# Where the scale and shift of two layer norms are worked out in a one-core attention and experts kernel

## What is computed

```python
def _layernorm(x, axis=-1, eps=1e-05):
    m = jnp.mean(x, axis=axis, keepdims=True)
    v = jnp.var(x, axis=axis, keepdims=True)
    return (x - m) / jnp.sqrt(v + eps)
...
x = x + jnp.tanh(g_xattn[0]) * _L0_xattn_ref(_layernorm(x, axis=-1), ctx_1024, ctx_1024, mask, Wq, Wk, Wv, Wo, 16)
x = x + jnp.tanh(g_ffn[0]) * _L0_ffn_ref(_layernorm(x, axis=-1), Wg, bg, W1, b1, W2, b2)
```

## Time and profile before

| | us |
|---|---|
| median of 3 runs | 1108.44 |
| lowest and highest run | 1108.04, 1109.18 |
| the profiled execution's own time | 1107.66 |
| its span on the core | 1105.6 |

### The profile page before, as it was taken

One profiled execution on the slowest core, in us unless ns is written; L12 is line 12 of the kernel. 1 busy time (PEld: TensorE's weight loads), 2 busy tenths in 40 slices (PEclk: granted clock), 3 DMA queues, 4 the chain that ended last, 5 costly groups with the idle time before them and its releaser, 6 DMA issues.

```text
span 1105.6 us, 36301 instructions
## 1 busy us (share of the span) xinstructions
PE 1024.9 (93%) x13797; PEld 755.4 (68%) x13797; DVE 894.4 (81%) x1803; ACT 943.1 (85%) x1809; POOL 791.7 (72%) x719
## 2 busy tenths in 40 slices
PE   5868799999999999999999999999999999999887
PEld 4446567776777777677777767777776777777655
DVE  2686688897888889788888978888897888787766
ACT  3988788889898888989888898988889898887865
POOL 3566667776867777686777768777776877788843
PEclk9999899999999999999999999999999999999999
DMA  9122121212112121211212121121212111111100
GB/s 219 33 56 59 49 56 43 55 45 59 50 40 57 52 57 43 59 50 40 57 52 56 43 59 50 40 57 52 54 45 59 50 31 46 44 40 50 29 3 20
DMA packets 123162, 56.90 MB, mean 51 GB/s; under 512 B 26584, under 2 KB 122864, under 8 KB 122992
## 3 DMA queue, kind: packets, MB, share of 16 engines
q1 hardware_dynamic: 122992, 54.59, 19.3%
HBM read 16.80 MB, written 4.19 MB: 19 GB/s over the span
## 4 chain that ended last, share of the span: by engine, by line
PE 49%; DVE 14%; ACT 12%; issue 12%; POOL 11%; DMA 1%; ACTq 0%; DVEq 0%; SPq 0%; POOLq 0%
PE bank L44 15%; PE bank L46 14%; PE bank L45 14%; POOL hidL L895 3%; POOL ptL L932 3%; ACT qH L464 3%; POOL rstd L880 3%; PE bank L307 2%; ACT bank L520 2%; PE bank L262 2%; DVE shift L668 2%; ACT x2hat L508 1%; DVE comb L868 1%; ACT vH L559 1%; DVE above L844 1%
## 5 line engine op out<-in xcount | busy, mean ns | idle before, releaser
L895 POOL TENSOR_TENSOR hidL<-hid,hidH 128x512 f16<-128x512 f32 x242 | 278.6, 1164 | 21.3 <-ACT hidH L494 21.3
L932 POOL TENSOR_TENSOR ptL<-pt,ptH 128x512 f16<-128x512 f32 x128 | 148.5, 1160 | 179.4 <-ACT pt L579 179.4
L675 DVE TENSOR_TENSOR qL<-bank,qH 128x512 f16<-128x512 f32 x224 | 153.4, 685 | 57.1 <-ACT qH L464 53.7
L484 ACT ACTIVATE hid<-bank,b1col 128x512 f32<-128x512 f32 x256 | 185.6, 725 | 8.3 <-PE bank L46 8.2
L494 ACT ACTIVATE hidH<-bank,b1col 128x512 f16<-128x512 f32 x256 | 188.3, 736 | 0.0
L464 ACT ACTIVATE qH<-bank 128x512 f16<-128x512 f32 x256 | 155.1, 609 | 36.0 <-PE bank L46 35.0
L44 PE MATMUL bank<-w2H,hidH 128*128 128x128 f16 x1024 | 179.0, 220 | 5.8 <-DVE hidL L788 5.2
L46 PE MATMUL bank<-w2H,hidL 128*128 128x128 f16 x1024 | 179.1, 220 | 0.0
L45 PE MATMUL bank<-w2L,hidH 128*128 128x128 f16 x1024 | 179.1, 220 | 0.0
L927 POOL TENSOR_TENSOR x<-x,y_scaled 128x512 f32<-128x512 f32 x114 | 146.0, 1280 | 14.1 <-DVE x L746 14.1
L938 POOL TENSOR_TENSOR prob<-prob,row_inv 128x512 f32<-128x512 f32 x128 | 133.4, 1043 | 15.2 <-DVE row_inv L782 15.2
(11 more groups left out here) (143 smaller groups left out, 3607.3 us busy)
## 6 DMA issues: line engine op xcount, KB each, us to landing
vdH<-vH SPq DMA_DIRECT2D x256, 64.0 KB, 2.1
vdL<-vL SPq DMA_DIRECT2D x256, 64.0 KB, 2.1
x_raw<-in_x SPq DMA_DIRECT2D x16, 256.0 KB, 3.0
ctx_raw<-in_ctx SPq DMA_DIRECT2D x16, 256.0 KB, 3.1
mask_raw<-in_fside_Bx1xSxS SPq DMA_DIRECT2D x32, 128.0 KB, 2.8
out_x<-x SPq DMA_DIRECT2D x16, 256.0 KB, 2.5
qH<-in_L_xattn_Wq SPq DMA_DIRECT2D x1, 512.0 KB, 6.0
qH<-in_L_xattn_Wk SPq DMA_DIRECT2D x1, 512.0 KB, 8.1
```

The costliest lines, as they stand in the source:

```text
L484: act.activation(hid[:, k % NR, :], bk("hid", g, e, c)[:, :], ACT.Relu, bias=b1col[:, e, c:c + 1]).then_inc(s_relu[c], 1)
L675: dve.tensor_tensor(qL[at], bk("Q", g, h)[:, :].rearrange("p (b q) -> p b q", b=GB), qH[at], ALU.subtract).then_inc(s_q_low[h % 2], 1)
L895: pool.tensor_tensor(hidL[:, m % 2, c, :], hid[:, k % NR, :], hidH[:, m % 2, c, :], ALU.subtract).then_inc(s_hid_low[c], 1)
L932: pool.tensor_tensor(ptL[:, b % 2, :], pt[:, b % 2, :], ptH[:, b % 2, :], ALU.subtract).then_inc(s_pt_low, 1)
```

## The change

The four small operations from the variance to the shift are all done on GpSimd, in one function, and `ln_var` and `ln_shift` on VectorE are gone. `scalar_tensor_tensor` (minus one times mean times rstd) becomes two operations, with a new tensor minus_mean between them. In the loop GpSimd does w = 0 at the end of step 4 as before, and w = 1 now at the end of step 4 too (step 5 before), behind w = 0.

```diff
+        minus_mean = sb("minus_mean", [P, 2, GT])
...
-            def ln_var(w, g):
-                dve.wait_ge(s_ln[w]["aggr"], g + 1)
-                dve.tensor_scalar(rstd[:, w], meanvar[:, w, :, 1], EPS, None, ALU.add).then_inc(s_ln[w]["var"], 1)
-
-            def ln_shift(w, g):
-                dve.wait_ge(s_rstd[w], g + 1)
-                if g:
-                    dve.wait_ge(s_ln[w]["rows"], g)
-                dve.scalar_tensor_tensor(shift[:, w], meanvar[:, w, :, 0], -1.0, rstd[:, w], ALU.mult,
-                                         ALU.mult).then_inc(s_ln[w]["shift"], 1)
...
                     if i == 4 - sooner:
                         ln_aggr(0, g + 2)
-                        ln_var(0, g + 2)
-                    if i == 5 - sooner:
-                        ln_shift(0, g + 2)
                 if within(g - 1, GROUPS):
                     if i == 4:
                         ln_stats(1, g - 1, x2[:, (g - 1) % NX2], (s_res, GT * g))
                         ln_aggr(1, g - 1)
-                    if i == 5:
-                        ln_var(1, g - 1)
-                        ln_shift(1, g - 1)
...
-            def reciprocal_root(w, g):
+            def ln_scale_shift(w, g):
+                pool.wait_ge(s_ln[w]["aggr"], g + 1)
+                if g:
+                    pool.wait_ge(s_ln[w]["rows"], g)
+                pool.tensor_scalar(rstd[:, w], meanvar[:, w, :, 1], EPS, None, ALU.add).then_inc(s_ln[w]["var"], 1)
                 pool.wait_ge(s_ln[w]["var"], g + 1)
                 pool.tensor_tensor(rstd[:, w], rstd[:, w], minus_half[:, :], ALU.pow).then_inc(s_rstd[w], 1)
+                pool.tensor_scalar(minus_mean[:, w], meanvar[:, w, :, 0], -1.0, None, ALU.mult).then_inc(s_ln[w]["minus"], 1)
+                pool.wait_ge(s_rstd[w], g + 1)
+                pool.wait_ge(s_ln[w]["minus"], g + 1)
+                pool.tensor_tensor(shift[:, w], minus_mean[:, w], rstd[:, w], ALU.mult).then_inc(s_ln[w]["shift"], 1)
...
                 if within(g + 2, GROUPS) and i == 4 - sooner:
-                    reciprocal_root(0, g + 2)
-                if within(g - 1, GROUPS) and i == 5:
-                    reciprocal_root(1, g - 1)
+                    ln_scale_shift(0, g + 2)
+                if within(g - 1, GROUPS) and i == 4:
+                    ln_scale_shift(1, g - 1)
```

More of the change, by code:

```diff
@@ L167, in flamingo_block @@
         s_marked, s_mask_in = sem("score_banks_marked"), sem("mask_in_bank")
-        s_ln = [{k: sem(f"ln{w}_{k}") for k in ("stats", "aggr", "var", "shift", "rows")} for w in range(2)]
+        s_ln = [{k: sem(f"ln{w}_{k}") for k in ("stats", "aggr", "var", "minus", "shift", "rows")} for w in range(2)]
         s_logit_in, s_gt, s_eq, s_gmax, s_gshift = (sem(n) for n in ("logit_in", "gt", "eq", "gate_max", "gate_shift"))
@@ L686, in _ @@
             ln_aggr(0, 0)
-            ln_var(0, 0)
-            ln_shift(0, 0)
             for n in range(H // 4):
@@ L909, in _ @@
             pool.wait_ge(s_half, 1)
-            reciprocal_root(0, 0)
+            ln_scale_shift(0, 0)
             for s in range(FIRST, LAST):
```

## The result

| | before | after |
|---|---|---|
| median us (runs) | 1108.81 (4) | 1074.98 (4) |
| lowest, highest | 1108.04, 1109.26 | 1073.69, 1077.04 |
| profiled execution, its span | 1107.66, 1105.6 | 1077.04, 1075.3 |

The ratio of after to before is 0.9697, 95% interval 0.968 to 0.9715: 3.0% faster. The forecast was 1083 us with a range from 1076 to 1097.

What follows compares the result with a forecast made beforehand. TensorE was taken to bound the kernel, with some 2 us idle a group. 12 x 1.46 + 4.8 + 2.9 = 25.2 us off the profiled 1107.66 gave 1082.5, plus 0.8 for the median: 1083 us, range 1076 to 1097.

Steps and rivals of the forecast that it cites:

- The bound and the mechanism: Steady groups: TensorE bounds, and idles because ScalarE waits 1.46 us for the second norm's shift at the end of step 5.
- Gain of a group: Steady middle: with shifts ready in time, ScalarE and then TensorE run 1.46 us earlier in each of 12 groups.
- The 0.2 us of waiting for ScalarE that I expected to remain: Step 6 of a group: between 0 and 0.4 us of TensorE's waiting for ScalarE stays, taken as 0.2.
- x: GpSimd's added time per norm, three small operations and two waits: 0.71 us, between 0.47 and 3.2.
- The 0.5 us to spare: End of step 4: 2.4 us more in GpSimd's queue fits the 2.9 us of room ahead of hidL for half 1.
- The sign named for dear operations: Profile after: TensorE's w2 times hid waiting for GpSimd's hidL in step 5 would show the small operations are dear.
- The place that I named as the narrowest: GpSimd's queue ahead of hidL for half 1, end of step 4: TensorE needs it for the expert's output; room 2.97 us.
- The start: Starting phase: two ScalarE waits before xhat, 2.79 and 2.01 us, both counted whole as 4.8 us gained.
- The end: End of program: TensorE's idle time at two norms, 2.9 us, counted as gain; upper bound 8.8; last norm nothing.
- The first one's condition: Rival: GpSimd's small operations cost 0.4 to 0.54 us each, delaying hidL for half 1; 1094 us; chance 12%.
- The slower one: Rival: hidL for half 1 comes too late behind GpSimd's queue, from 0.54 us an operation; about 1138 us; chance 8%.
- The third: Rival: TensorE's second idle time (0.81 us, x2hat transposes) has another cause, only 0.50 us a group counts; 1095 us; 7%.
- the fourth: Rival: nothing changes, as the second norm's statistics come late and GpSimd stands waiting; chance 3% with other small causes.

Runs made afterwards that it cites:

- move_only: Kernel before, operations left on their engines, but the second norm's epsilon addition and power done at the end of step 4 instead of step 5; 1085.1 us, ratio 0.9782.
- hidL_first: Changed kernel with the second norm's chain one place later in GpSimd's queue, behind hidL for half 1 of step 5; 1078.1 us, ratio 0.9716.
- dose4: Changed kernel with four more 128x4 multiplications on GpSimd ahead of the second norm's chain, results not used; 1087.5 us, ratio 0.9816.
- start_only: Kernel before with the change only for the first norm of groups 0 to 3 and the second norm of group 0; 1099.6 us, ratio 0.9926.
- again: The changed kernel unaltered, run once more for a second profile and more rounds; 1075.5 us, ratio 0.9704.
- spread: Changed kernel with the first norm's statistics, chain and rows one step earlier from group 1 on; 1070.7 us, ratio 0.9656.
- engine_only: Changed kernel with the second norm's chain on GpSimd at the end of step 5 instead of step 4; 1115.8 us, ratio 1.0062 to the kernel before.
- again_2: The changed kernel unaltered, run beside the version with the first norm one step earlier, on the same chip; 1076.1 us, ratio 0.9709.
- spread_again: The changed kernel with the first norm one step earlier from group 1 on, run a second time beside the changed kernel; 1071.0 us, ratio 0.9663.
- middle_only: Kernel before with the change only for the first norm of groups 4 to 15 and the second norm of groups 1 to 12; 1087.6 us, ratio 0.9818.
- tail_only: Kernel before with the change only for the last three norms (second norm, groups 13 to 15); 1102.4 us, ratio 0.9945.

## Why the prediction was right, and where it was off

The change did what was forecast, for the reason given, but the time fell out of the range at its lower end. What failed is the size of all three terms of the sum, each taken from recorded idle time and each too small, and the step from the profiled execution to the median.

**The bound and the mechanism** were right. TensorE's idle time behind ScalarE's wait went, and move_only shows that it was the wait inside step 5 and not the load of small operations on VectorE, which were all still there. Part of the round trip's length had a cause that I had not seen, VectorE's wait beside GpSimd (last section).

**Gain of a group: 1.46 predicted, 1.55 to 1.59 measured.** The step that failed is the duration: 1.46 us is ScalarE's recorded idle time, between the end of xhat and the start of x2hat. But its instructions start before the one ahead has ended (four xhat take 1.70 us and x2hat starts 1.54 behind them), so the idle time is 0.1 to 0.15 longer than recorded. From the start of xhat to the end of hidH it is 9.89 us before (509.19 to 519.08) and 8.33 after (495.30 to 503.63), 1.56 less. From sequence 16 to 112 the twelve groups win 18.9 us where 17.5 were summed, 1.4 more. The 0.2 us of waiting for ScalarE that I expected to remain shows where GpSimd doesn't hold TensorE first (0.19 us recorded in hidL_first).

**The added operations: x = 0.71 predicted.** Alone they were well taken: 0.23, 0.24 and 0.20 us where I took 0.18. What I mis-sized is what lies between them. The two chains and a hidL's length take 5.32 us from start to start; without the 2.11 that hidL and one power took, 3.21 us are added where the sum said 2.4, so x was 1.09 us. Behind the power and ahead of each dependent product stand 0.08 to 0.15 us of idle time. The 0.5 us to spare were therefore not there, and TensorE waits 0.38 us. The sign named for dear operations, w2 times hid waiting for hidL in step 5, is thus in the trace though the operations were cheap. It cost nothing, since ScalarE's path would have held TensorE as long (hidL_first). The place that I named as the narrowest was the right one; dose4 shows what each further us there costs. The Trainium skill (GPSIMD Engine Reference, Engine selection) has elementwise work about twice as slow on GpSimd with two inputs and roughly line-rate with one. The trace of this case doesn't bear out the factor of 2 at 128x4. The addition has one input, and took 0.23 us on GpSimd against 0.16 to 0.17 on VectorE where no large GpSimd operation ran beside it (before and move_only). The product has two, and took 0.20 us against 0.15 to 0.16 for VectorE's, which also multiplies by minus one. That is 1.3 to 1.4 times as long in both, and the 0.22 us that the rival doubled was itself lengthened by a GpSimd operation (last section).

**The start: 4.8 us predicted, 6.1 by the trace, 7.7 in start_only (0.8 of it there at the first sequence already).** The waits of 2.79 and 2.01 us were rightly counted. From sequence 8 to 16 after wins the 2.0 us of the second of them. The first one pays more than its 2.79, 4.1 us by sequence 8, although GpSimd's longer chain first makes the probability transposes of sequence 4 later by 1.9 us. A term that was missing is TensorE's clock. Before, TensorE idled there for 4.24 us from 78.4 us on, and in that stretch its clock fell to the lower of its two levels (1.2 GHz; granted 0.96 from 75 to 80 us, 0.50 from 80 to 85). The same window of before, after and again (columns as in the earlier trace rows; the clock stands behind the busy times):

```profile
75.00:90.00 15.00, 9.35 (x118) 6.86 (x119) 9.29 (x17) 11.91 (x25) 5.30 (x5) 0.77 0.18 49
...
75.00:90.00 15.00, 12.88 (x183) 10.35 (x184) 10.74 (x20) 13.55 (x27) 9.37 (x9) 0.89 0.33 83
...
75.00:90.00 15.00, 12.31 (x185) 9.39 (x185) 11.45 (x21) 14.05 (x28) 9.70 (x10) 1.00 0.32 81
```

After, TensorE's longest wait there is 2.50 us, and the clock is lower for a shorter time, or not at all. The runs give this a price. With the changed start, sequences 2 to 8 win 4.0 to 4.1 us in the profiles with 0.89 (after, spread, engine_only) and 4.7 to 4.8 us in those with 1.00 (again, again_2, start_only, hidL_first, dose4, spread_again). Without it, 0.89 wins 0.5 us (middle_only) and 0.66 loses 0.7 (tail_only) against the 0.77 of before. So a step of 0.11 is worth 0.5 to 0.7 us; of the 1.2 us above 2.79 in after it explains about half, and some 0.5 us stay open. Why again keeps its clock behind the same wait (2.49 us) is open too.

**The end: 2.9 us predicted, 5.1 by the trace, 5.6 in tail_only.** I took TensorE's recorded waits. The norm at 963 us gave 1.7 us (1.4 counted), the one at 1020 us 1.9 (1.5 counted), and the last, which I had put at nothing, 1.1 us between the expert's outputs of steps 115 and 118. For the last norm I had expected GpSimd to wait for VectorE as before; but x2hat's wait went from 2.71 us (at 1063 us) to 1.65 (at 1033), 1.06 us less, which is what arrived. Another 0.8 us come between the outputs of steps 121 and 122, where no norm is made, and 0.2 are lost behind it. This too goes with the clock. The window of before and the same work in tail_only:

```profile
1080.00:1090.00 10.00, 10.00 (x101) 7.43 (x100) 7.88 (x15) 6.38 (x12) 3.62 (x3) 0.84 0.10 28
...
1076.00:1086.00 10.00, 9.48 (x106) 6.62 (x106) 9.66 (x17) 7.19 (x13) 4.49 (x3) 1.00 0.09 28
```

The 0.8 us are there in every run with 1.00 at that place, after and even engine_only among them, and missing in those with 0.83 (start_only, middle_only, spread). Why the two counted norms gave 0.3 to 0.4 us more than TensorE's recorded idle time wasn't traced.

**From the trace to the median: 0.8 us added, 2.1 should have been taken off.** The four executions of after took 1077.04, 1075.57, 1074.39 and 1073.69 us at mean granted clocks of 0.991, 0.994, 0.996 and 0.995: the one that was profiled was the longest, with the lowest clock. The executions of before were within 1.2 us. That is 2.9 of the 8 us by which the forecast was off; the trace gave 30.3 us of span against 25.2 summed, 5.1 us, of which 1.4, 1.3 and 2.2 are the terms above.

**The rivals.** The first one's condition, 0.4 us and more an operation, isn't met, though x came half way to its 1.48 us by the pauses between the operations. The slower one was a true mechanism with a price far too high: at 0.20 to 0.24 us an operation it doesn't decide, but engine_only, where GpSimd's queue does, came out slower than before. The third, that the second idle time has another cause, is out, and the fourth too: GpSimd never stood waiting for the second norm's statistics in the middle. The range was too narrow at its lower end, since I took terms from recorded idle time, which was below the cost wherever these runs measured it, put the last norm at nothing, and left out the clock and the spread between executions.

## What to carry to other kernels

A short chain that crosses engines costs the engine that consumes it whatever lies between the moment when its inputs are there and the moment when the last link is issued; moving the link's issue earlier is worth more than moving it to another engine, and moving the engine alone can lose. Before adding work to a queue, find the first result behind it that the bounding engine needs and how much earlier it is ready: here 2.97 us of room against 3.2 us of work. Idle time that a profile records understates what a wait costs when instructions of an engine overlap (1.46 us recorded, 1.56 by the starts); distances from start to start give the whole. Compare the granted clock of each stretch before putting a difference there down to the change.

## What the runs showed of the hardware that I had not expected

- GpSimd's arithmetic on 128x4 numbers is recorded with 0.225 us (addition with a constant), 0.24 us (multiplication with a constant) and 0.20 us (product of two); only the power is dear, 1.04 us. Four independent ones follow each other at 0.19 us (0.78 us for the four of dose4).
- A product that waits for an operation just ahead of it on GpSimd starts 0.15 us after that one's end, and the multiplication behind the power 0.08 us after it without any wait.
- A small VectorE operation that starts while a GpSimd operation on 128x512 is running, or up to 0.02 us ahead of one, ends with that one, 0.02 to 0.03 us behind it. This is so for 56 of the 64 epsilon additions and products of before, which take 0.22 to 1.20 us for it; the other 8 had none beside them at their start, or only its last 0.06 us, and take 0.15 to 0.17 us. Beside GpSimd's power, which is 128x4, the addition took 0.17 us in move_only. The two long ones of the earlier trace rows, 508.86 to 510.06 and 511.19 to 512.31, stand beside the two hidL here (GpSimd's timeline of before), and the 0.22 us of the earlier trace rows end 0.03 us behind prob:

```profile
501.28 1.04 POOL L938 TENSOR_TENSOR prob<-prob,row_inv 128x512 f32<-128x512 f32 x1
...
508.87 1.16 POOL L895 TENSOR_TENSOR hidL<-hid,hidH 128x512 f16<-128x512 f32 x1
510.14 1.02 POOL L880 TENSOR_TENSOR rstd<-rstd,minus_half 128x4 f32<-128x4 f32 x1
511.13 1.16 POOL L895 TENSOR_TENSOR hidL<-hid,hidH 128x512 f16<-128x512 f32 x1
```

  So about 0.96 us of the 1.46 us that ScalarE waited are the product's wait beside hidL (an estimate: 1.12 us less the 0.16 us that it takes alone). Why the two engines meet is not shown by these runs, and no run separates the product from hidL in step 5.
